# A mixture of experts on one core: blocks of 256 rows with the weights stationary, in place of blocks of 128 rows with the rows stationary

## What is computed

```
x = x + 0.5 * ffn(layernorm(x))      # half step 1, "f1"
x = x + attention(layernorm(x))      # 16 heads of 64, rotary, causal
x = x + 0.5 * ffn(layernorm(x))      # half step 2, "f2", same weights

ffn(h):  logits = h @ router_w.T                    # 8 experts
         the two largest logits of a token, softmax over those two -> weights
         out = sum over the two experts e of  weight_e * (silu(h @ gate_w[e].T) * (h @ up_w[e].T)) @ down_w[e].T
```

## Time and profile before

| | us |
|---|---|
| median of three runs | 1266.61 |
| profiled execution, device time | 1263.21 |
| its span in the trace | 1261.5 |
| start of f1, up to the first product of block 0 | 52.4 |
| f1's blocks, up to the last down product | 205.9 |
| attention, up to the last residual and its statistics | 753.7 |
| start of f2 | 19.6 |
| f2's blocks, up to the last scatter | 208.1 |
| sums at the end | 21.8 |

### The profile page before, as it was taken

One profiled execution on the slowest core, in us unless ns is written; L12 is line 12 of the kernel. 1 busy time (PEld: TensorE's weight loads), 2 busy tenths in 40 slices (PEclk: granted clock), 3 DMA queues, 4 the chain that ended last, 5 costly groups with the idle time before them and its releaser, 6 DMA issues. The chain is left out here.

```text
span 1261.5 us, 28429 instructions
## 1 busy us (share of the span) xinstructions
PE 1196.3 (95%) x8838; PEld 912.5 (72%) x8838; DVE 905.5 (72%) x1995; ACT 791.4 (63%) x2264; POOL 814.1 (65%) x888
## 2 busy tenths in 40 slices
PE   7799999979999999999999999999999879999992
PEld 6588888856667666666667667766666668888881
DVE  6775344468888888888888997798998767533543
ACT  4665665656667666667667667767666656555552
POOL 4233356259888788788787787677666437666662
PEclk8899999989999999999999999999999969999996
DMA  9135122122221222122212222211221051113223
GB/s 323 32 96 155 57 56 70 42 69 56 62 53 42 60 60 50 44 60 54 57 46 51 62 64 51 60 43 43 52 49 37 18 184 43 47 50 113 62 63 110
DMA packets 87758, 86.54 MB, mean 69 GB/s; under 512 B 11248, under 2 KB 78704, under 8 KB 87232
## 3 DMA queue, kind: packets, MB, share of 16 engines
q1 hardware_dynamic: 76640, 65.50, 20.1%
q0 software_dynamic: 8864, 18.17, 5.2%
q10 hardware_dynamic: 2112, 1.05, 0.3%
HBM read 33.43 MB, written 17.69 MB: 41 GB/s over the span
## 5 line engine op out<-in xcount | busy, mean ns | idle before, releaser
L1915 POOL TENSOR_SCALAR at_prob<-at_prob,at_rec 128x128 f32<-128x128 f32 (+3 forms) x256 | 311.8, 1223 | 154.2 <-DVE at_rec L2126 152.3
L2306 ACT ACTIVATE at_prob<-at_s,at_nb 128x128 f32<-128x128 f32 (+3 forms) x512 | 264.7, 535 | 16.8 <-DVE at_nb L2118 13.4
L2317 ACT ACTIVATE at_probT<-at_pt 128x128 f32<-128x128 f32 (+3 forms) x256 | 105.2, 437 | 223.5 <-PE at_pt L2022 223.1
L790 POOL DMA_INDIRECT f_xb<-xn_dram,f_source x142 | 141.2, 994 | 160.4 <-PE f_b L1285 100.3
L2118 DVE TENSOR_REDUCE at_nb<-at_s 128x2 f32<-128x256 f32 (+3 forms) x256 | 203.5, 816 | 7.8 <-PE at_s L2008 7.8
L1447 DVE TENSOR_TENSOR f_hid<-f_b,f_silu 128x512 f32<-128x512 f32 x142 | 98.5, 693 | 135.8 <-PE f_b L1298 99.6
L2022 PE MATMUL at_pt<-ident,at_prob 128*128 128x128 f32 x1280 | 183.1, 275 | 5.5 <-DVE at_probT L2140 1.6
L2112 DVE TENSOR_TENSOR at_turned<-at_pj,rope 128x1024 f32<-128x1024 f32 x122 | 148.9, 1220 | 44.7 <-PE at_pj L1969 41.7
L2003 PE MATMUL at_s<-at_KT,at_QT 64*128 64x128 f32 (+3 forms) x1024 | 175.2, 460 | 5.2 <-DMA at_KT<-at_probT 2.8
L1909 POOL TENSOR_TENSOR at_R<-at_turned 128x512 f32<-128x512 f32 x126 | 157.4, 1268 | 24.0 <-DVE at_turned L2112 24.0
L2022 PEld LDWEIGHTS at_pt<-ident,at_prob 128*128 128x128 f32 x1280 | 140.9, 141 | 26.9 <-issue 15.5
(11 more groups left out here) (326 smaller groups left out, 2220.1 us busy)
## 6 DMA issues: line engine op xcount, KB each, us to landing
at_QT<-at_R SPq DMA_DIRECT2D x128, 128.0 KB, 2.4
at_KT<-at_R SPq DMA_DIRECT2D x124, 128.0 KB, 2.4
ys_dram<-y SPq DMA_DIRECT2D x71, 64.0 KB, 1.7
f_down<-down_t SPq DMA_DIRECT2D x2, 2048.0 KB, 9.3
xn_dram<-f_xn SPq DMA_DIRECT2D x12, 256.0 KB, 6.7
f_xb<-xn_dram,f_source POOLq DMA_INDIRECT x142, 2.5
X<-x SPq DMA_DIRECT2D x4, 512.0 KB, 6.2
gate<-gate_t SPq DMA_DIRECT2D x8, 256.0 KB, 5.1
```

What stands on the lines that cost most here:

```text
L790: pool.indirect_dma_start(out=xb[j % AHEAD][:, :], out_offset=None, in_=xn_dram, in_offset=bass.IndirectOffsetOnAxis(ap=routing.source[:, ...
L1915: pool.tensor_scalar(w, w, rec[:, q, 1:2], None, ALU.mult).then_inc(probB_ready, 1)
L2306: act.activation(prob[q][:, h, :], s_bank[q % 2][:, h, 0:n], ACT.Exp, bias=nb[:, q, h:h + 1], scale=1.0, accum_out=sums[:, q, h:h + 1]).th ...
L2317: act.activation(probT[0][:, 0:q + 1, q * P:(q + 1) * P], pt_bank[0][:, at:at + (q + 1) * P].rearrange("p (b r) -> p b r", r=P), ACT.Copy) ...
```

## The change

Blocks have 256 rows (`WIDE = 2`), and there are 39 of them (32, and 7). The lead part is 20 tiles, the later part 12. In `project` the operands change places: 128 columns of an expert's weights are stationary and 256 rows stream past, so gate and up come out with the hidden dimension on the partitions, hid needs no turning, and a block takes 24 passes of 256 columns in two halves. The next block's rows are turned between the halves. Gate, up and down stay in SBUF as loaded, in float32; for each block ACT copies its expert's high parts (`leading_weights`, 1024 numbers per partition) and DVE subtracts for the low parts (`trailing_weights`), two blocks and one block ahead. The splitting at the start, the parking of up's low parts and the second load of down are gone.

```diff
+WIDE = 2
+OUTPUTS = 3
-        LEAD = 16
+        LEAD = 20
...
         def gather(pool, j):
             pool.wait_ge(routing.lists_ready, routing.SOURCES[j >= SURE])
-            pool.indirect_dma_start(
-                out=xb[j % AHEAD][:, :], out_offset=None, in_=xn_dram,
-                in_offset=bass.IndirectOffsetOnAxis(ap=routing.source[:, j:j + 1], axis=0)
-            ).then_inc(xb_in[j % AHEAD], 16)
+            for t in range(WIDE):
+                c = WIDE * j + t
+                pool.indirect_dma_start(
+                    out=xb[j % AHEAD][:, t, :], out_offset=None, in_=xn_dram,
+                    in_offset=bass.IndirectOffsetOnAxis(ap=routing.source[:, c:c + 1], axis=0)
+                ).then_inc(xb_in[j % AHEAD], 16)
...
+        def keep_warm(pe, count):
+            for _ in range(count):
+                pe.transpose(bank[5][:, 0:P], ident[:, :], ident[:, :])
...
+                        for c in range(4):
+                            routing.find(pe, 0, c, found_bank)
+                            keep_warm(pe, 12)
...
-                def project(j, k, e):
+                def project(j, halves):
+                    k = j % 2
                     pe.wait_ge(xlo_ready, j + 1)
-                    wait(pe, hid_ready, j - 1)
...
-                    hi, lo = xt[k][:, 0, :], xt[k][:, 1, :]
-                    for w, o in ((gate, gate_bank[k]), (up, up_bank[k])):
...
-                        pe.matmul(o[:, :], hi, wh, start=True, stop=False)
-                        pe.matmul(o[:, :], hi, wl, start=False, stop=False)
-                        one = pe.matmul(o[:, :], lo, wh, start=False, stop=True)
-                        one.then_inc(gu_psum, 1)
+                    pe.wait_ge(wlo_ready, j + 1)
+                    x_hi, x_lo = xt[k][:, 0, :], xt[k][:, 1, :]
+                    for z in halves:
+                        for g, into, reader in ((0, gate_bank[z], silu_ready), (1, up_bank[z], hid_ready)):
+                            wait(pe, reader, 2 * (j - 1) + z + 1)
+                            for c in range(2):
+                                cols = slice((2 * z + c) * P, (2 * z + c + 1) * P)
+                                o = into[:, c * ROWS:(c + 1) * ROWS]
+                                pe.matmul(o, w_hi[k][:, g, cols], x_hi, start=True, stop=False)
+                                pe.matmul(o, w_hi[k][:, g, cols], x_lo, start=False, stop=False)
+                                one = pe.matmul(o, w_lo[k][:, g, cols], x_hi, start=False, stop=True)
+                            one.then_inc(gu_psum, 1)
...
+                keep_warm(pe, 20)
+                for j in range(-1, BLOCKS + 1):
...
+                    if has(j, 0):
+                        project(j, (0,))
+                    if has(j, 1):
+                        turn_rows(j + 1)
+                    if has(j, 0):
+                        project(j, (1,))
...
+                    if has(j, -1):
+                        project_down(j - 1)
...
+                for j in range(-1, BLOCKS + 1):
+                    if has(j, 1) and j >= 0:
+                        trailing_weights(j + 1)
+                    if has(j, 0):
+                        hidden(j, 0)
+                    route_later(j)
...
+                    if has(j, 0):
+                        hidden(j, 1)
+                    if has(j, 1):
+                        trailing_rows(j + 1)
...
-        LEAD_NORMED = {LEAD_FACTORS + n: g for g, n in enumerate((5, 6, 8, 9))}
+        LEAD_NORMED = {LEAD_FACTORS + n: g for g, n in enumerate((5, 6, 8, 9, 10))}
-        LEAD_CHOSEN = LEAD_FACTORS + 11
-        LEAD_COUNTED = LEAD_FACTORS + 17
+        LEAD_CHOSEN = LEAD_FACTORS + 12
+        LEAD_COUNTED = LEAD_CHOSEN + 4
```

More of the change, by code:

```diff
@@ L592, in targets, with sevens, seven_owners @@
         dve.tensor_scalar(self.target[:, some], spot, -1.0, None, ALU.add).then_inc(self.lists_ready, 1)
+    def sevens(self):
+        first, sevens = 0, []
+        while first < self.blocks:
+            r = 0 if first < self.sure else 1
+            start = min(first, self.windows[r].stop - 1)
+            stop = min(start + 7, self.sure if r == 0 else self.blocks)
+            sevens.append((r, start, range(first, stop)))
+            first = stop
+        return sevens
+    def seven_owners(self, eng, r, start):
+        eng.wait_ge(self.lists_ready, self.OWNERS[r])
+        packed = eng.value_load(self.owners[0:1, start:start + 1], min_val=0, max_val=self.E ** 7 - 1)
+        return [packed // self.E ** d % self.E for d in range(7)]
     def owned(self, r):
@@ new lines, in project_down @@
+                def project_down(j):
+                    k, e = j % 2, owner(j)
+                    pe.wait_ge(hid_ready, 2 * j + 2)
+                    wait(pe, y_ready, j)
+                    if lead is None and j == 0:
+                        pe.wait_ge(down_in, 16)
+                    for t in range(WIDE):
+                        rows = slice(t * P, (t + 1) * P)
+                        for c in range(FC):
+                            one = pe.matmul(y_bank[:, rows], hidT[k][:, c, rows],
+                                            down[:, bass.ds(e, 1), c, :].rearrange("p a d -> p (a d)"),
+                                            start=(c == 0), stop=(c == FC - 1))
+                    one.then_inc(y_psum, 1)
@@ new lines, in _, with leading_weights @@
+                owner = Owners(act)
+                def leading_weights(j):
+                    if lead is None and j == 0:
+                        act.wait_ge(gate_up_in, 16 * 2 * E)
+                    e = owner(j)
+                    wait(act, gu_psum, 4 * (j - 2) + 4)
+                    act.activation(w_hi[j % 2][:, :, :],
+                                   gate_up[:, bass.ds(e, 1), :, :].rearrange("p a g f -> p (a g) f"),
+                                   ACT.Copy).then_inc(whi_ready, 1)
```

679 lines of the change are left out of this document (305 added, 374 removed).

## The result

The changed kernel takes 1292.04 us (median of 4 runs, 1289.31 to 1292.66) against 1265.68 for the kernel before on the same chip: ratio 1.0203 [1.0176, 1.0231], 26 us slower. The forecast was 1271, some 5 us slower. The profiled execution took 1291.45 us (before: 1263.21), its span is 1289.7 (before: 1261.5). Ratios are formed of executions in the faster of two states that the chip shows; a fourth execution of the sixth experiment, 1926.84 us, was in the slower one and is left out.

The account below looks back on a forecast made before the run. TensorE was taken to bound the loops, a chain of small steps the starts; -6.9 - 4.0 + 7.1 + 6.5 + 3.1 - 1.4 = +4.4 on 1263.2 gave 1267.6, as a median 1271 us (own range 1262 to 1283; 8 of 10 within 1249 to 1293).

Parts of the forecast that it names:

- rival of shared reading: TensorE's loops: weight load and stream share their reading, a pass costs 0.135, total 1301 (1292 at 0.130); chance 0.16.
- p: Time of one 256-column gate or up pass on TensorE, in us: 0.119 taken, range 0.112 to 0.135.
- the last rival: TensorE's loops: weight loads aren't hidden at all, a pass costs 0.224, total 1468; chance 0.01.
- The starts: Stretches before each half step's loop: f1 +7.1 us, f2 +6.5, with f2's first pass 26 us after the attention's end.
- the attention: Between the loops: a fifth lead group +1.5 us and packing the lead part's owners +1.6, together +3.1.
- f1's start: Before f1's loop: statistics +0.9 us, fifth group +2.3, lists +4.0, search -1.6, a block's rows +1.5; together +7.1.
- The routing waits: TensorE waiting for later-part routing between a block's products: 4.4 us per loop; f1's first-sequence preparation (blocks 34, 35) adds 1.9.
- f2's loop: Second half step's loop: 204 us against 208.1 (-4.0), POOL just hidden behind TensorE, a wait of 2 at block 30.
- The third rival: f2's loop: POOL sets the pace, 5.08 us per block, loop ends at 208 instead of 204, total 1275; chance 0.08.
- f1's loop: First half step's loop: 189.4 us of blocks plus 9.6 of waits and ends, 199.0 against 205.9 (-6.9).
- the first weights and the low clock: Term of 0.6 us in each half step's loop.
- The tail: After f2's last scatter: six instead of eight reads for the last sums, 0.71 us each to start; -1.4 us.

Follow-up runs that it names:

- sixth experiment: Changed kernel, but from f2's block 12 ACT copies weights to two PSUM banks and DVE subtracts from there; ratio 1.0136.
- fourth experiment: Changed kernel without the twelve transposes behind each quarter of the search, in both half steps; one run of 1283.3 us.
- fifth experiment: Changed kernel, but from f2's third block on DVE subtracts only 64 of 1024 columns for the weights' low parts; 1280.48 us.
- third experiment: Changed kernel with 44 instead of 20 transposes ahead of the first block's rows, in both half steps; one run of 1288.35 us.
- second experiment: Changed kernel without the second of each block's two scatters in f2, so half of the rows are not written; 1269.36 us.
- spread loads: The seventh experiment's kernel, with the reads for f2's lead sums made to wait for earlier sums instead of starting in one go; 1271.87 us.
- seventh experiment: Changed kernel with low weights by PSUM from f2's block 12, no transposes in the search, and f2's lead sums from block 32; 1275.32 us.

## Why the prediction was right and where it failed

**The number.** It was forecast that the kernel would get slower, and it did. But 1292 is above the forecast's own range (1262 to 1283) and inside the wide one (1249 to 1293) by 1 us, and that is luck: the wide range reached so high for the rival of shared reading, which has 1292 at p = 0.130, and p came out at 0.119. What did put the time there had a price of 1275 and a chance of 0.08.

**Right.** The pass's price, on which most of its argument went: 0.119. So the rule on weight loads from "TensorE: Matmul & The Clock Gate" in the Trainium skill (section "The mechanism", list "What overlaps and what doesn't"), which made the last rival, does not hold here for 256-column passes either. The starts (+6.7 for +7.1; 26.27 for 26) and the attention came out. In f1's start the terms did so one by one, by DVE's rows: the first decision begins at 24.50 instead of 21.54 (+3.0, predicted 3.2), the lists end at 47.52 instead of 40.97 (+3.6 from there, predicted 4.0), what was found is copied at 50.86 instead of 45.59 (-1.3 for -1.6), and from there to the first pass it takes 1.5 more, as predicted. The fourth experiment shows that the search is indeed on the chain. The routing waits of f1's blocks 1 to 10 are 6.3 for 5.6 with the search, and those around block 34 are 1.9 for 1.9.

**Failed: f2's loop.** The step is "so POOL ends near 196 to 199 after it and is just hidden behind TensorE", with a wait of 2 at block 30. The sum of 204 against the 222.3:

| term | predicted | measured |
|---|---|---|
| 39 blocks | 189.4 | 190.1 |
| waits of the first twelve blocks | 6.2 | 8.4 |
| waits for y buffers, blocks 19 to 29 | 0 | 5.2 |
| blocks 30 and 31 | 2 | 12.2 |
| last pass to last scatter | 6 | 6.2 |

Two things were wrong in it. The 1.27 per DMA was taken from rows in which nothing held POOL, while the change itself puts a two-operand step of 1.23 us beside it in every block: 15.9 of the 17.3 us of held issues. Removing them gives back 9.7 us (fifth experiment), or 9.9 behind block 12 alone (sixth), with the spread said above. I had costed the subtraction on DVE and ACT only; the trace of before had 7 held issues to read the price from, and the page of the Trainium skill named above states the rule. And POOL was compared with TensorE by its end alone. A sum over the loop hides that from block 12 on POOL is slower in every block (5.12 against 4.875) and already late by then, beside the later part's lists and its own two list products (a lag of 5.8 at block 10 in the fifth experiment), so that its scatters are late in the middle of the loop, where y buffers and sums ask for them. Per 256 rows the kernel before left POOL 2 x 2.84 = 5.68 us for the same four DMAs.

The third rival, POOL's pace, had the mechanism, y buffers and the sums' reads included, and blocks 21 to 23 do take its 5.12; its price of 208 took an average pace for the loop and no wait with a queue behind it. The wait in block 30 costs so much because DVE's queue is in order: 8.94 us for a read became 9.88 for TensorE. What gives most of the 18 back is shown by runs: 202.0 with half the scatters, 207.5 with all of them, none held by the subtraction behind block 12, later sums and spread reads.

**Failed by less: f1's loop**, 4.4 short: 0.7 for the block (4.875 for 4.856), 0.7 in the routing waits, 1.5 in the first block, 1.5 at the end (predicted 1.5, is 3.0: an output copy waited for and the second half's down products). For the first weights and the low clock the sum had 0.6, and the first block takes 2.1 over the usual. The third experiment has 0.9 of it left at the full clock, which is the cover missing in the first block, a term that the sum left out; the other 1.2 go with the low clock, which the prediction had too small.

**The tail** did not get its 1.4: the first of the last reads starts 6.2 us after the last scatter's end, before 4.8. In the second experiment, with one scatter per block, it is 3.1 and the tail 18.3, so the second scatter of a block has part in it; by what way is open, since no run was made for it.

**What stays of the change.** With f2's loop mended (207.5 against 208.0), the two starts and the attention still cost 12.3 us more than before in the trace of the spread loads, and f1's loop gives back 3.0, which is why no version beats the kernel before.

## What to carry to other kernels

When a change makes the engine that bounds a loop faster, compare every other in-order engine with the new period block by block, not by its sum at the end: one that is 5% too slow fails in the middle, where buffers run out and where something stands in another queue behind its results. A new DVE step with two SBUF operands is also a cost on POOL if POOL issues indirect DMAs beside it; read its other operand from PSUM, or keep it short. Reads that were spread by the pace of a loop should stay spread when they are moved to its end.

## What the runs showed of the hardware

- An indirect DMA issued by POOL under a DVE step with two SBUF operands lasts what is left of that step plus 0.82 to 0.90 us (up to 2.04 instead of 0.97, 27 issues of the changed kernel); with one operand in PSUM it isn't held (27 issues of the sixth experiment, 0.96 to 1.00).
- A scatter of 128 rows landed 2.3 us after its issue in the loop, and 5.2 to 8.3 in the seventh experiment while the sums' reads moved some 300 GB/s.
- 256-column passes with a weight load of 0.19 each follow each other at 0.12 (in f1's loop), 8-column passes at 0.113.
